# Rows written before the second experts carry their own shift and inverse deviation, and six row gathers go ahead of the six record gathers

## The chip, the cores and the metric

The kernel runs on one core of a Trainium2 chip. The metric is the device time of one execution in microseconds (us); the time of a kernel is the median over several runs. Five engines work beside each other: PE multiplies matrices (PEld loads its weights), DVE and ACT do elementwise work, POOL does small elementwise work and issues the indirect transfers (gathers and scatters), SP issues the plain ones. They meet only at semaphores: an instruction waits until a counter has reached a value.

## The reference

The input is 4096 tokens of 256 numbers. Three blocks follow each other, each on the layer norm of its input and added to it:

```python
x = L0_attn_u
x = x + 0.5 * _L0_ffn_ref(_layernorm(x), Wr, W1, b1, W2, b2)   # mixture of 8 experts
x = x + _L0_attn_ref(_layernorm(x), A_real, A_imag, B, C)      # a linear recurrence over the tokens
x = x + 0.5 * _L0_ffn_ref(_layernorm(x), Wr, W1, b1, W2, b2)   # the same experts again
# _layernorm: (x - mean) / sqrt(var + 1e-5)
# _L0_ffn_ref: the router picks argmax(x @ Wr) of 8 experts and the largest softmax probability p;
#              out = p * (gelu(x @ W1[e] + b1[e]) @ W2[e] + b2[e])
# _L0_attn_ref: h_t = a * h_{t-1} + B u_t (128 complex states), y_t = Re(C h_t)
```

## The kernel before, in words

Tokens are sorted by expert. Each of the two expert stages (`ph` 1 and 2) works through `NT` = 39 tiles `q` of up to 128 sorted tokens: a gather fetches the tile's rows into `xg[q % 6]`, a second gather fetches four numbers for each token, its record (shift, inverse deviation, half the probability), into `recf[:, q % 6]`. Then, for each tile, ACT normalises (`norm`), PE turns the tile (`turn_tile`), ACT and DVE scale and split it into two half-precision parts (`high_x`, `split_x`), PE multiplies by the first weights (`product1`), ACT applies gelu, DVE splits again (`split_h`), PE multiplies by the second weights (`product2`), DVE adds bias and the old row (`result`), and POOL scatters the new rows to DRAM. `RING` = 6 gathers are in flight. `result(q)` writes into `og[q % 2]`, so it waits until the scatter of tile q-2 has landed.

Between the two expert stages lies the recurrence, over 8 chunks `c` of 512 tokens (4 columns of 128 tokens each): SP loads the rows that the first experts wrote (`x1_dram`, rows of `RW` = 258 numbers: the last two are the mean and variance), DVE runs the scan, `add_y(c)` adds the output to the rows in `xs` (for the last chunk ACT does, in `squares`), ACT takes sums of squares (`squares(c)`), and SP stores the new rows to `x2_dram` as soon as they are added (`s_x2`). POOL makes the scan's carried state after each chunk, and in `second_norm` the inverse deviation (a `pow`) and the shift. These stand in `records`, which DVE completes with the probability (`route_weigh`) and SP stores (`store_records`). `route_odds` on DVE waits for `second_norm` of all tokens.

The order on each engine is the order in which the code is written. Toward the second experts it is this. POOL: `second_norm` of the last chunk (after `tile_slots(2)`), then in `ffn` the wait for the sorted order (`sorted_sb`) and for all stores of rows (`s_stored`), and then in pairs the row gather and the record gather of tiles 0 to 5; the first record gather waits for the stored records:

```python
                    for to, source, index in ((xg[k], table, 0), (recf[:, k, :], rec_dram[ph], 1)):
                        if index == 1 and q == 0:
                            pool.wait_ge(s["sorted_all"], 1)
                            pool.wait_ge(s["rec_stored"], 16)
```

Both gathers of a tile count on one semaphore, and `norm(q)` waits for both. PE meanwhile runs matrix products whose results nobody reads (`idle`, L1178): 12 of them after `route_sort(2)`, 5 after the first `turn_tile`.

## Time and profile before

| what | value |
| --- | --- |
| median of 3 runs (lowest to highest) | 613.54 us (612.56 to 614.28) |
| time of the profiled execution | 613.17 us |
| its span | 611.4 us |
| PE busy | 551.8 us (90% of the span) |
| DVE busy | 467.6 us (76%) |
| ACT busy | 409.8 us (67%) |
| POOL busy | 288.1 us (47%) |
| first experts, all 39 tiles | from about 93 us to 306 us of the span |
| recurrence and second routing | about 306 us to 397 us |
| second experts | about 397 us to the end |

The time is 1.8 us more than the span; what lies around the span is not in the trace. A busy share is an average over stages. What an edit is worth is read at the place where it sits: which wait ends last there, and what runs meanwhile.

### The profile page before, as it was taken

To read this page: it belongs to the slowest core of one execution; us is meant where nothing else is said; L and a number is where in the kernel's file an instruction comes from. 1 tells how busy PE (TensorE), PEld (TensorE's weight loads), DVE (VectorE), ACT (ScalarE), POOL (GpSimd) and SP (SyncE) were. 2 spreads that over 40 slices of the span, in tenths; PEclk is the share of its full clock that TensorE was granted. 3 is DMA by queue.
4 is the path that set the end of the run, shared out by engine and by line. 5 is a ranking of instruction groups with operands and counts; after the bars stand their busy time and mean duration, and the time that the engine had idled before them with its cause. 6 is when DMAs were issued, how large, how long until landed. Compare 5 with 4: busy or idle time off the path is not lost.

```text
span 611.4 us, 18700 instructions
## 1 busy us (share of the span) xinstructions
PE 551.8 (90%) x6548; PEld 508.6 (83%) x6548; DVE 467.6 (76%) x1007; ACT 409.8 (67%) x966; POOL 288.1 (47%) x326
## 2 busy tenths in 40 slices
PE   5992158999999999999989989699999999999996
PEld 5991047999999999999977767699999999999996
DVE  5789997888887788877749998666677666666674
ACT  3899977676667776676455662387766677766763
POOL 0025075655655555653245142655555555545532
PEclk9555569999999999999999996799999999999999
DMA  7999112211111121111081223111111112111210
GB/s 250 369 370 378 33 26 97 62 47 55 54 45 55 37 52 44 46 47 36 16 278 35 93 80 104 58 46 54 52 48 53 51 48 45 46 46 46 52 30 15
DMA packets 34873, 51.94 MB, mean 85 GB/s; under 512 B 6747, under 2 KB 27933, under 8 KB 34528
## 3 DMA queue, kind: packets, MB, share of 16 engines
q1 hardware_dynamic: 24800, 31.93, 15.3%
q0 software_dynamic: 9984, 18.83, 11.4%
q8 instruction: 56, 0.92, 0.6%
q14 instruction: 33, 0.27, 0.2%
HBM read 37.98 MB, written 14.59 MB: 86 GB/s over the span
## 4 chain that ended last, share of the span: by engine, by line
PE 67%; DVE 11%; issue 6%; DMA 6%; SPq 4%; POOL 4%; ACT 1%; POOLq 0%; DVEq 0%; ACTq 0%
PE banks L1270 30%; PE banks L1292 10%; PE banks L1293 10%; PE banks L1294 10%; DVE weights_arena L1124 3%; PE banks L1245 3%; DMA weights_arena<-L_attn_u 2%; PE banks L1200 2%; SPq L330 2%; DMA weights_arena<-x_after_ffn 2%; DVE weights_arena L1133 1%; POOL weights_arena L424 1%; DVE weights_arena L1121 1%; SPq L313 1%; DVE weights_arena L1105 1%
## 5 line engine op out<-in xcount | busy, mean ns | idle before, releaser
L617 ACT ACTIVATE weights_arena<-banks,b1t,inv 128x128 f32<-128x128 f32 (+7 forms) x624 | 220.1, 459 | 31.3 <-PE banks L1270 31.2
L1270 PE MATMUL banks<-weights_arena 128*128 128x128 f16 (+7 forms) x3744 | 207.0, 215 | 1.2 <-DVE weights_arena L950 1.1
L1270 PEld LDWEIGHTS banks<-weights_arena 128*128 x3744 | 199.9, 98 | 3.5 <-issue 2.5
L1292 PE MATMUL banks<-weights_arena 128*128 (+7 forms) x624 | 170.3, 273 | 0.2 <-issue 0.2
L1294 PE MATMUL banks<-weights_arena 128*128 (+7 forms) x624 | 170.2, 273 | 0.0
L1293 PE MATMUL banks<-weights_arena 128*128 (+7 forms) x624 | 170.2, 273 | 0.0
L964 DVE TENSOR_SCALAR weights_arena<-weights_arena,hscale 128x512 f16<-128x512 f32 (+5 forms) x156 | 74.7, 479 | 76.0 <-ACT weights_arena L617 75.2
L967 DVE SCALAR_TENSOR_TENSOR weights_arena<-weights_arena,hscale 128x512 f16<-128x512 f32 (+5 forms) x156 | 109.9, 704 | 5.6
L591 ACT ACTIVATE weights_arena<-banks,xscale 128x256 f16<-128x256 f32 (+7 forms) x78 | 35.5, 455 | 90.7 <-PE banks L1245 90.7
L424 POOL DMA_INDIRECT recf<-records,sorti x78 | 76.9, 986 | 23.8 <-issue 23.8
L430 POOL DMA_INDIRECT out<-weights_arena,sorti x39 | 39.5, 1014 | 78.4 <-DVE weights_arena L984 70.6
L430 POOL DMA_INDIRECT x_after_ffn<-weights_arena,sorti x39 | 39.9, 1024 | 77.0 <-DVE weights_arena L988 68.6
L1292 PEld LDWEIGHTS banks<-weights_arena 128*128 128x128 f16 (+7 forms) x624 | 62.3, 100 | 7.0 <-issue 0.7
L1294 PEld LDWEIGHTS banks<-weights_arena 128*128 128x128 f16 (+7 forms) x624 | 62.3, 100 | 6.5
L1293 PEld LDWEIGHTS banks<-weights_arena 128*128 128x128 f16 (+7 forms) x624 | 62.3, 100 | 5.7
L424 POOL DMA_INDIRECT weights_arena<-L_attn_u,sorti x39 | 46.2, 1184 | 29.0 <-DVE sorti L928 17.4
L575 ACT ACTIVATE weights_arena<-weights_arena,recf 128x256 f32<-128x256 f32 (+7 forms) x78 | 46.0, 590 | 8.8 <-DMA recf<-records,sorti 8.8
L981 DVE SCALAR_TENSOR_TENSOR weights_arena<-banks,inv,weights_arena 128x256 f32<-128x256 f32 (+7 forms) x78 | 37.6, 483 | 16.1 <-issue 5.9
L424 POOL DMA_INDIRECT weights_arena<-x_after_ssm,sorti x39 | 40.0, 1026 | 15.1 <-issue 11.6
L950 DVE SCALAR_TENSOR_TENSOR weights_arena<-banks,xscale,weights_arena 128x256 f16<-128x256 f32 (+7 forms) x78 | 35.6, 457 | 7.8 <-ACT weights_arena L591 7.0
L984 DVE SCALAR_TENSOR_TENSOR weights_arena<-weights_arena,recf 128x256 f32<-128x256 f32 (+7 forms) x78 | 37.8, 484 | 2.8
L729 DVE SCALAR_TENSOR_TENSOR weights_arena<-weights_arena,wscale 128x2048 f16<-128x2048 f32 x16 | 37.1, 2341 | 2.3 <-ACT weights_arena L516 2.3
(216 smaller groups left out, 639.1 us busy)
## 6 DMA issues: line engine op xcount, KB each, us to landing
weights_arena<-L_ffn_W SPq DMA_DIRECT2D x16, 1024.0 KB, 12.6
weights_arena<-x_after_ffn SPq DMA_DIRECT2D x8, 516.0 KB, 8.4
weights_arena<-L_attn_u SPq DMA_DIRECT2D x8, 512.0 KB, 10.8
x_after_ssm<-weights_arena SPq DMA_DIRECT2D x8, 512.0 KB, 2.9
weights_arena<-L_ffn_b SPq DMA_DIRECT2D x2, 1024.0 KB, 5.2
recf<-records,sorti POOLq DMA_INDIRECT x78, 2.5
weights_arena<-L_attn_u,sorti POOLq DMA_INDIRECT x39, 3.3
x_after_ffn<-weights_arena,sorti POOLq DMA_INDIRECT x39, 2.5
```

Of the source, the lines that this page charges most:

```text
L424: pool.indirect_dma_start(to, None, source, bass.IndirectOffsetOnAxis(ap=sorti[:, slot(q), index:index + 1].bitcast(U32), axis=0)).then_in ...
L430: pool.indirect_dma_start(dst, bass.IndirectOffsetOnAxis(ap=sorti[:, slot(q), 2:3].bitcast(U32), axis=0), og[q % 2] if ph == 1 else og[q % ...
L575: act.activation(xng[q % 2][0:w], xg[q % RING][0:w], ACT.Identity, bias=recf[0:w, q % RING, 0:1], scale=recf[0:w, q % RING, 1:2]).then_inc ...
L617: last = act.activation(hb[q % 2][:, f, 0:width(q)], src, ACT.Gelu, bias=b1t[:, bass.ds(e * FC + f, 1)], scale=inv1[:, bass.ds(e, 1)])
L964: dve.tensor_scalar(hs[q % 2][:, 0, f, of], hb[q % 2][:, f, of], sc, None, ALU.mult) \
L967: dve.scalar_tensor_tensor(hs[q % 2][:, 1, f, of], hb[q % 2][:, f, of], sc, hs[q % 2][:, 0, f, of], ALU.mult, ALU.subtract).then_inc(s["hs ...
L981: dve.scalar_tensor_tensor(o, acc, i2, b2b[0:w, bass.ds(e * D, D)], ALU.mult, ALU.add) \
L984: last = dve.scalar_tensor_tensor(o, o, recf[0:w, q % RING, 2:3], xg[q % RING][0:w], ALU.mult, ALU.add)
L1270: last = pe.matmul(acc[:, f * P:f * P + n_cols], weights[wpart * DC + d], xts[q % 2][:, xpart, d, 0:n_cols], start=(n == 0), stop=(n == 5))
L1292: pe.matmul(acc, hs[q % 2][:, 0, f, of], high, start=(f == 0), stop=False)
L1293: pe.matmul(acc, hs[q % 2][:, 0, f, of], low, start=False, stop=False)
L1294: last = pe.matmul(acc, hs[q % 2][:, 1, f, of], high, start=False, stop=(f == FC - 1))
```

## The change

The rows in `x2_dram` become 258 numbers long: `second_norm` runs once for each chunk and puts shift and inverse deviation behind the chunk's rows in `xs`. SP's store of a chunk waits for it (`s_nb2`) as well. In the second experts `norm` takes both numbers from the gathered row, and so it waits for the row gather alone; the record gathers count on semaphores of their own, and only `result` waits for them (`records_landed`). At the start of the second experts POOL issues six row gathers and then six record gathers. In both stages `og` has six buffers instead of two, and a few buffers have other addresses.

```diff
--- before.py
+++ after.py
@@ -80,7 +80,7 @@
     x1_dram = nc.dram_tensor("x_after_ffn1", [T, RW], F32, kind="Internal").ap()
 
     rec_dram = {ph: nc.dram_tensor(f"records_{ph}", [T, 4], F32, kind="Internal").ap() for ph in (1, 2)}
-    x2_dram = nc.dram_tensor("x_after_ssm", [T, D], F32, kind="Internal").ap()
+    x2_dram = nc.dram_tensor("x_after_ssm", [T, RW], F32, kind="Internal").ap()
     ctx = ExitStack()
     with ctx:
         def sb(name, shape, dt=F32):
@@ -175,12 +175,12 @@
         hb = [view(k * 1024, FC, P) for k in range(2)]
         b2b = view(2048, E * D)
         hs = [view(4096 + k * 1024, 2, FC, P, dt=F16) for k in range(2)]
-        og = [view(6144 + k * RW, RW) for k in range(2)]
-        xg = [view(8192 + k * D, D) for k in range(RING)]
-        xng = [view(9728 + k * D, D) for k in range(2)]
+        og = [view(6144 + k * RW, RW) for k in range(RING)]
+        xg = [view(8192 + k * RW, RW) for k in range(RING)]
+        xng = [view(10752 + k * D, D) for k in range(2)]
         xts = [view(10240 + k * 256, 2, DC, P, dt=F16) for k in range(2)]
 
-        outcols = [view(6912 + k * D, DC, P) for k in range(2)]
+        outcols = [view(12288 + k * D, DC, P) for k in range(2)]
 
         xs = view(0, NJ, RW)
         uns = [view(NJ * RW + k * CT * D, CT, D) for k in range(2)]
@@ -248,6 +248,8 @@
                 "xt_hi xt m1 gelu h_hi hsplit m2 o_chain o").split()}
             S[ph]["gath"] = [sem(f"gath{k}_{ph}") for k in range(RING)]
             S[ph]["scat"] = [sem(f"scat{k}_{ph}") for k in range(RING)]
+        row_gath = {1: S[1]["gath"], 2: S[2]["gath"]}
+        record_gath = {1: S[1]["gath"], 2: S[1]["gath"]}
         s_load = [sem(f"s_load{k}") for k in range(NC)]
         s_nb, s_un, s_ut, s_uts, s_g, s_mod, s_hr, s_y, s_lg, s_nm, s_x2, s_sq, s_nb2, s_scan, s_neg, s_lx, s_prod, s_state, s_ext = (
             sem(n) for n in ("s_nb s_un s_ut s_uts s_g s_mod s_hr s_y s_lg s_nm s_x2 s_sq s_nb2 s_scan s_neg s_lx s_prod s_state s_ext").split())
@@ -282,6 +284,10 @@
         def in_slot(k):
 
             return len(range(k, NT, RING))
+
+        def records_landed(q):
+
+            return 32 * in_slot(q % RING) + 16 * (q // RING + 1)
 
         def weight_parts(e, which):
 
@@ -367,7 +373,8 @@
                 sp.dma_start(xs[:, c * CT:(c + 1) * CT, :], x1_chunks[c]).then_inc(s_load[c], 16)
             for c in range(NC):
                 sp.wait_ge(s_x2, c + 1)
-                sp.dma_start(x2_chunks[c], xs[:, c * CT:(c + 1) * CT, 0:D]).then_inc(s_stored[2 * c // NC], 16)
+                sp.wait_ge(s_nb2, c + 1)
+                sp.dma_start(x2_chunks[c], xs[:, c * CT:(c + 1) * CT, :]).then_inc(s_stored[2 * c // NC], 16)
                 if c == NC - 2:
                     load_b2(2)
             store_records(2)
@@ -412,31 +419,41 @@
                     for k in range(2):
                         pool.wait_ge(s_stored[k], 16 * (NC // 2))
 
-                def fetch(q):
-
-                    k = q % RING
+                def fetch_rows(q):
+
                     if q >= RING:
                         pool.wait_ge(s["o"], q - RING + 1)
-                    for to, source, index in ((xg[k], table, 0), (recf[:, k, :], rec_dram[ph], 1)):
-                        if index == 1 and q == 0:
-                            pool.wait_ge(s["sorted_all"], 1)
-                            pool.wait_ge(s["rec_stored"], 16)
-                        pool.indirect_dma_start(to, None, source, bass.IndirectOffsetOnAxis(
-                            ap=sorti[:, slot(q), index:index + 1].bitcast(U32), axis=0)).then_inc(s["gath"][k], 16)
+                    to = xg[q % RING][:, 0:D] if ph == 1 else xg[q % RING]
+                    pool.indirect_dma_start(to, None, table, bass.IndirectOffsetOnAxis(
+                        ap=sorti[:, slot(q), 0:1].bitcast(U32), axis=0)).then_inc(row_gath[ph][q % RING], 16)
+
+                def fetch_records(q):
+
+                    if q == 0:
+                        pool.wait_ge(s["sorted_all"], 1)
+                        pool.wait_ge(s["rec_stored"], 16)
+                    pool.indirect_dma_start(recf[:, q % RING, :], None, rec_dram[ph], bass.IndirectOffsetOnAxis(
+                        ap=sorti[:, slot(q), 1:2].bitcast(U32), axis=0)).then_inc(record_gath[ph][q % RING], 16)
 
                 def scatter(q):
 
                     pool.wait_ge(s["o"], q + 1)
                     pool.indirect_dma_start(dst, bass.IndirectOffsetOnAxis(ap=sorti[:, slot(q), 2:3].bitcast(U32), axis=0),
-                                            og[q % 2] if ph == 1 else og[q % 2][:, 0:D], None, bounds_check=T - 1, oob_is_err=False) \
+                                            og[q % RING] if ph == 1 else og[q % RING][:, 0:D], None, bounds_check=T - 1, oob_is_err=False) \
                         .then_inc(s["scat"][q % RING], 16)
 
                 for q in range(RING):
-                    fetch(q)
+                    fetch_rows(q)
+                    if ph == 1:
+                        fetch_records(q)
+                if ph == 2:
+                    for q in range(RING):
+                        fetch_records(q)
                 for q in range(NT):
                     scatter(q)
                     if q + RING < NT:
-                        fetch(q + RING)
+                        fetch_rows(q + RING)
+                        fetch_records(q + RING)
 
             tile_slots(1)
             ffn(1, u, x1_dram)
@@ -452,11 +469,14 @@
                 pool.tensor_tensor(nb[:, of], nb[:, of], rs[:, of], ALU.mult).then_inc(s_nb, 1)
                 pool.tensor_tensor(sd[:, of], rs[:, of], var1[:, of], ALU.mult).then_inc(s_nb, 1)
 
-            def second_norm(of):
-
+            def second_norm(c):
+
+                of = slice(c * CT, (c + 1) * CT)
+                pool.wait_ge(s_sq, c + 1)
                 chain.link(pool.tensor_scalar(m2[:, of], m2[:, of], 1.0 / D, EPS, ALU.mult, ALU.add))
                 chain.link(pool.tensor_tensor(rstd[:, of], m2[:, of], mhalf[:, of], ALU.pow))
-                pool.tensor_tensor(shift[:, of], nmean[:, of], rstd[:, of], ALU.mult).then_inc(s_nb2, 1)
+                pool.tensor_copy(xs[:, of, D + 1], rstd[:, of])
+                pool.tensor_tensor(xs[:, of, D], nmean[:, of], rstd[:, of], ALU.mult).then_inc(s_nb2, 1)
 
             zr, zi = zz[:, 0, CH - 1:CH], zz[:, 1, CH - 1:CH]
             cl, sl = turn[:, 0, CH - 1:CH], turn[:, 1, CH - 1:CH]
@@ -474,14 +494,12 @@
                 pool.tensor_tensor(state[:, 1:2], ev[:, 19:20], ev[:, 21:22], ALU.subtract).then_inc(s_state, 1)
                 if c == 0:
                     inverse_deviations(len(BATCHES) - 1)
-                if c == NC - 3:
-                    pool.wait_ge(s_sq, NC // 2)
-                    second_norm(slice(0, NJ // 2))
-            pool.wait_ge(s_sq, NC - 1)
-            second_norm(slice(NJ // 2, NJ - CT))
+                if c >= 2:
+                    second_norm(c - 2)
+            second_norm(NC - 3)
+            second_norm(NC - 2)
             tile_slots(2)
-            pool.wait_ge(s_sq, NC)
-            second_norm(slice(NJ - CT, NJ))
+            second_norm(NC - 1)
             ffn(2, x2_dram, out)
 
 
@@ -570,10 +588,12 @@
 
                     if q >= 2:
                         act.wait_ge(s["turned"], q - 1)
-                    act.wait_ge(s["gath"][q % RING], q // RING * 32 + 32)
+                    act.wait_ge(s["gath"][q % RING], (q // RING + 1) * (32 if ph == 1 else 16))
                     w = width(q)
-                    act.activation(xng[q % 2][0:w], xg[q % RING][0:w], ACT.Identity, bias=recf[0:w, q % RING, 0:1],
-                                   scale=recf[0:w, q % RING, 1:2]).then_inc(s["xn"], 1)
+                    row = xg[q % RING][0:w]
+                    moments = recf[0:w, q % RING, 0:2] if ph == 1 else row[:, D:RW]
+                    act.activation(xng[q % 2][0:w], row[:, 0:D], ACT.Identity, bias=moments[:, 0:1],
+                                   scale=moments[:, 1:2]).then_inc(s["xn"], 1)
 
                 experts = {}
 
@@ -834,7 +854,7 @@
             def route_odds(ph):
 
                 s = S[ph]
-                dve.wait_ge(a_nb if ph == 1 else s_nb2, 1 if ph == 1 else 3)
+                dve.wait_ge(a_nb if ph == 1 else s_nb2, 1 if ph == 1 else NC)
                 dve.tensor_tensor(je(rt[0]), je(rt[0]), over_e(rstd), ALU.mult).then_inc(s["diff"], 1)
 
             def route_count(ph):
@@ -973,19 +993,21 @@
                     if q == 0:
                         dve.wait_ge(s["b2in"], 16)
                     dve.wait_ge(s["m2"], q + 1)
-                    if q >= 2:
-                        dve.wait_ge(s["scat"][(q - 2) % RING], (q - 2) // RING * 16 + 16)
+                    if q >= RING:
+                        dve.wait_ge(s["scat"][q % RING], q // RING * 16)
+                    if ph == 2:
+                        dve.wait_ge(record_gath[ph][q % RING], records_landed(q))
                     w = width(q)
-                    o, acc = og[q % 2][0:w, 0:D], bank[4 + q % 2][0:w, 0:D]
+                    o, acc = og[q % RING][0:w, 0:D], bank[4 + q % 2][0:w, 0:D]
                     i2 = inv2[0:w, bass.ds(e, 1)]
                     dve.scalar_tensor_tensor(o, acc, i2, b2b[0:w, bass.ds(e * D, D)], ALU.mult, ALU.add) \
                         .then_inc(s["o_chain"], 1)
                     dve.wait_ge(s["o_chain"], q + 1)
-                    last = dve.scalar_tensor_tensor(o, o, recf[0:w, q % RING, 2:3], xg[q % RING][0:w], ALU.mult, ALU.add)
+                    last = dve.scalar_tensor_tensor(o, o, recf[0:w, q % RING, 2:3], xg[q % RING][0:w, 0:D], ALU.mult, ALU.add)
                     if ph == 1:
                         link(last)
                         link(dve.bn_stats(stats[0:w, q % 2, :], o))
-                        last = dve.bn_aggr(og[q % 2][0:w, D:D + 2], stats[0:w, q % 2, :])
+                        last = dve.bn_aggr(og[q % RING][0:w, D:D + 2], stats[0:w, q % 2, :])
                     last.then_inc(s["o"], 1)
 
                 for q in range(3):
```

The order of instructions moves at three places. First POOL, from the last `second_norm` on: `records` is shift and inverse deviation, `x_after_ssm` is `x2_dram`, `recf` takes the record gathers, `sorti` holds the indices. Before:

```order
L405 TENSOR_SCALAR weights_arena<-weights_arena 128x40 [waits pool_chain]
L457 TENSOR_SCALAR m<-m 128x4 [waits s_sq]
L458 TENSOR_TENSOR records<-m,mhalf 128x4 [waits pool_chain]
L459 TENSOR_TENSOR records<-nmean,records 128x4 [waits pool_chain]
L424 DMA weights_arena<-x_after_ssm,sorti 128x256 [waits s_stored1,s_stored0,sorted_sb_2]
L424 DMA recf<-records,sorti 128x4 [waits rec_stored_2,sorted_all_2]
L424 DMA weights_arena<-x_after_ssm,sorti 128x256
```

After:

```order
L412 TENSOR_SCALAR weights_arena<-weights_arena 128x40 [waits pool_chain]
L476 TENSOR_SCALAR m<-m 128x4 [waits s_sq]
L477 TENSOR_TENSOR records<-m,mhalf 128x4 [waits pool_chain]
L478 COPY weights_arena<-records 128x4 [waits pool_chain]
L479 TENSOR_TENSOR weights_arena<-nmean,records 128x4
L427 DMA weights_arena<-x_after_ssm,sorti 128x258 [waits s_stored1,s_stored0,sorted_sb_2]
L427 DMA weights_arena<-x_after_ssm,sorti 128x258 x5
L435 DMA recf<-records,sorti 128x4 [waits rec_stored_2,sorted_all_2]
L435 DMA recf<-records,sorti 128x4 x5
L441 DMA out<-weights_arena,sorti 4096x256 [waits o_2]
```

The last `second_norm` is one copy longer, and all six row gathers now stand ahead of the instruction that waits for the stored records. The five `second_norm`s of the earlier chunks, not shown, moved into the loop over the chunks, each after the state of the chunk two further on.

Second SP's queue over the recurrence: loads of rows, stores of rows, the bias `b2`, records. Before:

```order
L367 DMA weights_arena<-x_after_ffn 128x4x258 x7
L370 DMA x_after_ssm<-weights_arena 128x4x256 [waits s_x2] x7
L357 DMA weights_arena<-L_ffn_b 128x2048 [waits s_sq,s_stored0]
L370 DMA x_after_ssm<-weights_arena 128x4x256 [waits s_x2]
L361 DMA records<-records 128x128 [waits rec_ready_2]
```

After:

```order
L373 DMA weights_arena<-x_after_ffn 128x4x258 x7
L377 DMA x_after_ssm<-weights_arena 128x4x258 [waits s_nb2,s_x2] x7
L363 DMA weights_arena<-L_ffn_b 128x2048 [waits s_sq,s_stored0]
L377 DMA x_after_ssm<-weights_arena 128x4x258 [waits s_nb2,s_x2]
L367 DMA records<-records 128x128 [waits rec_ready_2]
```

Each store has one more wait, on POOL; nothing changes places.

Third DVE at the end of the first experts, the last two calls of `result` (tiles 37 and 38; `m2` is PE's second product, `scat` a landed scatter). Before:

```order
L981 ISA [waits scat5_1,m2_1]
L981 SCALAR_TENSOR_TENSOR weights_arena<-banks,inv,weights_arena 96x256
L984 SCALAR_TENSOR_TENSOR weights_arena<-weights_arena,recf 96x256 [waits o_chain_1]
L987 BN_STATS stats<-weights_arena 96x6 [waits dve_chain]
L988 BN_AGGR weights_arena<-stats 96x2 [waits dve_chain]
L981 ISA [waits scat0_1,m2_1]
L981 SCALAR_TENSOR_TENSOR weights_arena<-banks,inv,weights_arena 16x256
```

After:

```order
L1003 ISA [waits scat1_1,m2_1]
L1003 SCALAR_TENSOR_TENSOR weights_arena<-banks,inv,weights_arena 96x256
L1006 SCALAR_TENSOR_TENSOR weights_arena<-weights_arena,recf 96x256 [waits o_chain_1]
L1009 BN_STATS stats<-weights_arena 96x6 [waits dve_chain]
L1010 BN_AGGR weights_arena<-stats 96x2 [waits dve_chain]
L1003 ISA [waits scat2_1,m2_1]
L1003 SCALAR_TENSOR_TENSOR weights_arena<-banks,inv,weights_arena 16x256
```

Each waits for another scatter: tile 37 waited for that of tile 35 and now waits for that of tile 31, tile 38 for that of tile 32 in place of 36.

## Rows read from the trace of the kernel before

**Rows 1.** Stage table: stretch, its length, busy us by engine, PE clock, DMA.

```profile
397.00:600.00 203.00, 202.88 (x2809) 191.43 (x2809) 138.29 (x263) 143.04 (x380) 108.37 (x109) 1.00 0.17 46
```

**Rows 2.** Chain that ended last, 284 to 312 us: start, us, what.

```profile
303.64 2.11 DMA x_after_ffn<-weights_arena,sorti
305.86 0.38 SPq L367
```

**Rows 3.** Timeline of DVE: start, us, instruction, idle before and releaser.

```profile
299.52 0.48 DVE L981 SCALAR_TENSOR_TENSOR weights_arena<-banks,inv,weights_arena 96x256 f32<-96x256 f32 x1 [1.86 <-DMA x_after_ffn<-weights_arena,sorti]
301.22 0.47 DVE L981 SCALAR_TENSOR_TENSOR weights_arena<-banks,inv,weights_arena 16x256 f32<-16x256 f32 x1
...
606.39 0.47 DVE L981 SCALAR_TENSOR_TENSOR weights_arena<-banks,inv,weights_arena 16x256 f32<-16x256 f32 x1 [1.71 <-PE banks L1294]
```

**Rows 4.** Timeline of PE, last product of tile 38 in each expert stage.

```profile
300.46 0.27 PE L1294 MATMUL banks<-weights_arena 128*16 x1
...
605.94 0.27 PE L1294 MATMUL banks<-weights_arena 128*16 x1
```

**Rows 5.** Chain that ended last, 381 to 402 us.

```profile
386.97 0.21 POOL records L459
...
387.21 0.42 DVE weights_arena L838
...
390.21 0.20 DVE sorti L928
390.41 0.28 issue
390.69 0.46 POOL weights_arena L424
...
392.13 2.19 DMA recf<-records,sorti
...
394.33 0.61 ACT weights_arena L575
```

**Rows 6.** Timeline of PE before the second experts.

```profile
389.17 5.27 PE L1178 MATMUL banks<-iota_r,ident 128*128 128x128 f32 x24
394.99 0.44 PE L1245 MATMUL banks<-ident,weights_arena 128*128 128x128 f32 x2 [0.54 <-ACT weights_arena L575]
```

**Rows 7.** Timeline of SP, the last store of rows.

```profile
381.21 0.36 SPq L370 DMA_DIRECT2D x_after_ssm<-weights_arena x1
```

**Rows 8.** Tile `x_after_ssm`, 325 to 390 us: the eight stores of rows.

```profile
DMA to landing us min/median/max: 2.8/2.9/5.0
```

**Rows 9.** DMA, 335 to 341 us: queue (packets, MB, share), issue (us to landing).

```profile
q8 instruction: 1, 0.02, 1.9%
...
x_after_ssm<-weights_arena SPq DMA_DIRECT2D x1, 512.0 KB, 5.0
```

**Rows 10.** The same view, 363 to 368 us.

```profile
q8 instruction: 1, 0.02, 1.3%
...
x_after_ssm<-weights_arena SPq DMA_DIRECT2D x1, 512.0 KB, 4.2
```

**Rows 11.** The same view, 387.9 to 389.9 us: all packets of this stretch.

```profile
DMA packets 1, 0.02 MB, mean 8 GB/s; under 512 B 0, under 2 KB 0, under 8 KB 0
```

**Rows 12.** DMA, 380 to 402 us: the first row gathers.

```profile
weights_arena<-x_after_ssm,sorti POOLq DMA_INDIRECT x5, 2.8
```

**Rows 13.** Timeline of POOL: norm of 16 columns, state of chunk 6, norm of 4 columns.

```profile
356.82 0.94 POOL L457 TENSOR_SCALAR m<-m 128x16 f32<-128x16 f32 x1 [0.67 <-ACT banks L659]
...
362.97 0.19 POOL L474 TENSOR_TENSOR state<-ev 128x1 f32<-128x1 f32 x1
...
385.40 1.49 POOL L458 TENSOR_TENSOR records<-m,mhalf 128x4 f32<-128x4 f32 x1
```

**Rows 14.** Timeline of DVE: turn of the last chunk, which needs that state.

```profile
365.32 1.22 DVE L1121 TENSOR_TENSOR weights_arena<-turn,banks 128x1024 f32<-128x1024 f32 x1
```

**Rows 15.** Stage table around the start of the second experts.

```profile
391.00:393.00 2.00, 2.00 (x12) 2.00 (x11) 1.09 (x4) 0.00 (x0) 1.70 (x2) 0.50 0.22 59
395.00:397.00 2.00, 1.54 (x12) 1.35 (x12) 0.48 (x1) 0.47 (x1) 1.53 (x2) 1.00 0.28 71
```

## The prediction

> **What bounds the kernel now.** I read the stage table first: within the second experts PE is busy 202.88 of 203.00 us at the full granted clock [rows 1], so nothing that the change does to gathers or buffers inside a stage can save time there. What is left are the seams, where the chain of waits leaves PE. There are two that the change touches. The first is the end of the first experts: the chain runs over the landing of a scatter to DVE's `result(37)` and `result(38)`, over the last scatter, which lands at 303.64 + 2.11 = 305.75, and to SP's first load at 305.86 [rows 2, 3]. The second is the start of the second experts: last `second_norm` on POOL until 387.18, `route_odds`, sorting, the sorted order at 390.41, a row gather, the record gather of tile 0, which starts at 392.13 and lands at 394.32, and ACT's first `norm` at 394.33 [rows 5]. PE's first turn follows at 394.99, after 0.54 us of idleness [rows 6]. All terms below are worked out on the clock of this trace; they add.
>
> **End of the first experts: -0.3.** `result(37)` stood 1.86 us waiting for the scatter of tile 35 [rows 3]. With six buffers it waits for one landed long ago, so it starts when PE has delivered, and is out of the way of `result(38)`. That one can then start when PE's last product is there. PE's last matmul ended at 300.46 + 0.27 = 300.73 [rows 4]. How long DVE needs from there is to be seen at the end of the second experts, where nothing else holds it: 605.94 + 0.27 = 606.21 to 606.39, so 0.18 [rows 3, 4]. 300.91 instead of 301.22 is 0.31 earlier. Scatter, landing and SP's loads all hang on it in the chain [rows 2]. Of the 1.86 us only this is left, because PE is late next. Ends: nothing (if the loads gain nothing from starting earlier) and -0.5 (no latency at all, 301.22 - 300.73). At the end of the second experts nothing is gained: `result(38)` there waited 1.71 us for PE, not for a scatter [rows 3].
>
> **Recurrence: 0.** The old norm of 16 columns sat in front of the state of chunk 6 from 356.82 on; that state was done at 363.16 and DVE asked for it only at 365.32 [rows 13, 14], 2.2 us of slack even then. The new norms have 4 columns; the `pow` of one takes 1.49 us [rows 13], with the smaller instructions about 2.5 us, one per chunk, each behind the state it could delay. Even if each instruction ran at the price of the 0.94 row instead of a few tenths, it would be shorter than the old one from 356.82. If that cover were gone, every microsecond of late state would move the kernel by one. SP's later stores and the bias load behind them are not needed before the first gather and the first `result`. Ends: 0 and 0.
>
> **Last norm: +0.2 on what follows it.** One copy of 4 columns is added, priced as the neighbouring instruction of that shape, 0.21 [rows 5]. DVE's `route_odds` starts 0.02 us after the old end, so sorting and everything behind it on DVE and PE moves with it: the sorted order comes at 390.6, and POOL, which needed 0.28 us from there to its gather [rows 5], could issue at 390.9.
>
> **The last store of rows: the term on which the sum turns.** It went out at 381.21 [rows 7], 0.03 us after ACT's copy; it was more than 6 us ahead of being needed. Now it waits for the shift and goes out at 387.4. Of the eight stores the median landed 2.9 us after issue [rows 8]: 390.3, just ahead of the sorted order at 390.6, so hidden by 0.3 us. But one took 5.0 and one 4.2. The two have something in common: in their stretch lies a packet of the instruction queue, 0.02 MB [rows 9, 10]. The stretch in which the new store would move its data, from half a microsecond after its issue to half a microsecond before the usual landing (387.9 to 389.9), has today exactly one packet, 0.02 MB [rows 11], the size of that kind. PE's instructions are the same in number and order after the change, and at that point PE waits for DVE, so the packet should move with them by the same 0.2 us and meet the store. Then the landing takes 4.2 to 5.0 us; I take the middle, 4.6, between the two. 387.4 + 4.6 = 392.0; POOL's gather starts 0.28 later, at 392.3; the row gather lands 2.8 us later [rows 12], at 395.1, against 394.32 for the record of today. `norm` takes 0.61, and PE's turn moves from 394.99 to 395.7: **+0.7**. Ends: landing 2.9 and 5.0.
>
> The Trainium skill speaks against this term: in "Runtime: NRT & Kernel Launch", section "Instruction fetch mechanics", an engine's instructions come in 16 KiB blocks over a DMA queue of its own, and the cost of crossing to the next block is called mostly hidden. By that rule the store would land as the median does. The two slow stores say otherwise for a transfer that shares the time with such a block, and "DMA: Bandwidth & Descriptors", section "Why a DMA increments its semaphore by 16 and not by 1", gives a reason that fits them: a transfer is spread over up to 16 engines and counts as landed only with the last one. By the first rule alone the sum would be that of the first rival below; by the rows it is the one forecast.
>
> **What the gain would have been.** Leaving the record out of `norm`'s wait takes away 1.44 us between the two gathers (390.69 to 392.13) and changes a 2.19 us landing for one of 2.8 [rows 5, 12]: without the store's delay the row is there at 390.9 + 2.8 = 393.7 and normalised at 394.3. PE could not use all of it: its 24 idle passes, at a granted clock of 0.50 [rows 15], ended at 394.44 [rows 6] and now end 0.2 later, 394.6. So the turn would come at 394.6 and not at 394.99, **-0.35**. These passes cap the step.
>
> **Records: 0.** The record of tile 0 is now the seventh gather, 6 x 1.44 = 8.6 us after the first, so at 400.9, and lands about 2.2 later at 403.1 [rows 5]. `result(0)` follows three half tiles of PE's work: 203 us hold some 37 tiles [rows 1], so 5.5 each, 397.8 + 8.2 = 406. If this cover of 3 us were gone, DVE would hold `product2(2)` through the bank, not earlier. Further down one more wait for each `result` lies in DVE's idle time, except in the last one, where it may cost 0.05.
>
> **Sum.** -0.3 + 0 + 0.7 + 0.05 = +0.4 on the profiled execution's 613.17 (span 611.4 and 1.8 around it): **613.6 us**. The median of the runs shown, 613.54, lies 0.4 above that execution, so the same sum on the median would be 614.0; 613.6 is as good as these can tell apart. 0.3% of the time, what a measurement of this kernel can tell from no change, is 1.84 us.
>
> **Rivals.** *First: the store is hidden after all* (the packet comes earlier or later than the store's data, or costs nothing). Then -0.31 - 0.35 + 0.05 = -0.6: 612.6. For it: the median of the eight stores, 2.9, hardly above the least, 2.8 [rows 8]; against it: the packet in the stretch. The edge is a landing of about 3.8 us: below it PE's turn is earlier than today, above it later. A mild form of this is that the change doesn't do what it says: rows go ahead, but PE's idle passes end only 0.5 us before today's turn, so there is little to win in any case.
>
> *Second, on the slower side: the new wait lowers PE's clock.* Between the idle passes and the first turn PE now stands 1.1 us in place of 0.54. The granted clock was 0.50 (the lower of the two levels, 1.2 GHz) over 391 to 393 and 1.00 over 395 to 397 [rows 15]. If it fell again at the longer gap for about the length of the idle passes, which ran at that level for 5 us [rows 6], PE would do half its work in them: 2.5 us, with the 0.4 of the sum 616.1. The point from which it decides is whether the clock falls at all after 395. Against it: five more idle matmuls follow the first turn at once.
>
> *Third: more is won than I see*, for instance if, with the first seam's wait gone, all of its 1.86 us [rows 3] came back and the store were hidden too: -1.86 - 0.35 = -2.2, 611.0. Against it stands PE's last product at 300.73.
>
> **How the numbers follow.** The forecast 0.62, first rival 0.25, second 0.07, third 0.06. Range of the likeliest: landing 4.2 gives +0.0, 5.0 gives +0.8, a gain of nothing at the first seam +0.3 more, so 613.2 to 614.3; with the scatter of runs (612.56 to 614.28 for one kernel) and the first rival, 611.9 to 614.8. Faster by over 0.3% needs 611.7: the third rival and a little of the first, 0.07. Slower needs 615.4: the second rival and a little more, 0.08. Within 0.3%: 0.85.
>
> **What would show it.** Right: `result(37)` without a wait for a scatter and SP's first load 0.3 us earlier; a last store that lands over 4 us after issue, with an instruction packet in its stretch; POOL's first row gather released by the store and not by the sorted order; PE's first turn more than 0.54 us after the idle passes. Wrong: a landing of 2.9 (then 612.6), a granted clock below 1.00 after the first product, or a wait of `result` for a record.

## The result, and the profile after

The changed kernel took **616.0 us** (median of five executions, 613.66 to 617.71), beside 613.5 us (612.56 to 614.28) for the kernel before on the same chip: ratio 1.004, 95% interval 1.002 to 1.0059. That is 2.5 us above the median of before. The profiled execution took 615.49 us with a span of 613.1, against 613.17 and 611.4.

The chain of waits of the changed kernel, 284 to 320 us and then 375 to 415 us (start, us, what), answers to [rows 2, 5]:

```profile
304.20 2.11 DMA x_after_ffn<-weights_arena,sorti
306.43 0.38 SPq L373
...
386.13 1.50 POOL records L477
387.69 0.19 POOL weights_arena L478
387.88 0.18 POOL weights_arena L479
388.13 4.08 DMA x_after_ssm<-weights_arena
392.27 0.76 issue
393.03 2.92 DMA weights_arena<-x_after_ssm,sorti
395.98 0.61 ACT weights_arena L595
396.63 0.45 PE banks L1267 x2
```

DVE and the sorting have left the chain. It now runs from POOL's last norm to SP's store, through a landing of 4.08 us, to POOL, to the landing of the first row gather, to ACT and PE. The timelines say the same from the engines' side (start, us, instruction, idle time before and its releaser): DVE's `result(37)`, its two `result(38)`, the gather, PE's idle passes and PE's first turn; they answer to [rows 3, 6].

```profile
299.08 0.48 DVE L1003 SCALAR_TENSOR_TENSOR weights_arena<-banks,inv,weights_arena 96x256 f32<-96x256 f32 x1 [0.52 <-PE banks L1316]
301.79 0.47 DVE L1003 SCALAR_TENSOR_TENSOR weights_arena<-banks,inv,weights_arena 16x256 f32<-16x256 f32 x1 [1.04 <-PE banks L1316]
...
608.04 0.47 DVE L1003 SCALAR_TENSOR_TENSOR weights_arena<-banks,inv,weights_arena 16x256 f32<-16x256 f32 x1 [1.72 <-PE banks L1316]
...
393.03 1.12 POOL L427 DMA_INDIRECT weights_arena<-x_after_ssm,sorti  x1 [4.98 <-DMA x_after_ssm<-weights_arena]
...
390.06 5.39 PE L1200 MATMUL banks<-iota_r,ident 128*128 128x128 f32 x24
396.63 0.44 PE L1267 MATMUL banks<-ident,weights_arena 128*128 128x128 f32 x2 [1.19 <-ACT weights_arena L595]
```

The DMA view of the changed kernel, 387 to 389 us (packets; queue with packets, MB, share; issue with KB and us to landing), answers to [rows 9, 10]:

```profile
DMA packets 1, 0.02 MB, mean 8 GB/s; under 512 B 0, under 2 KB 0, under 8 KB 0
...
q8 instruction: 1, 0.02, 3.7%
...
x_after_ssm<-weights_arena SPq DMA_DIRECT2D x1, 516.0 KB, 4.1
```

The instruction packet is there, in the stretch of the store, as forecast. The stage table of the changed kernel (length; busy us of PE, PEld, DVE, ACT, POOL; granted clock; DMA share, GB/s) answers to [rows 1, 15]:

```profile
40.00:78.00 38.00, 12.27 (x79) 10.80 (x79) 35.71 (x73) 35.58 (x32) 12.04 (x9) 1.00 0.64 224
...
395.00:397.00 2.00, 0.81 (x6) 0.60 (x6) 0.00 (x0) 0.60 (x1) 1.39 (x3) 0.94 0.38 114
397.00:600.00 203.00, 202.34 (x2789) 190.93 (x2788) 137.21 (x261) 142.92 (x380) 109.87 (x110) 1.00 0.18 47
```

**Where the time went.** I cut each traced execution at four marks that every kernel has: POOL's first gather of the first experts, DVE's last `result(38)` there, PE's first turn of the second experts, and the last `result(38)`. The lengths are differences of the starts in the timelines; the last 5 us of a span are alike in all.

```
                          to the first   first     from result(38)  second   span
                          gather         experts   to PE's turn     experts
before                    78.21          223.01    93.77            211.40   611.4
changed                   79.10          222.69    94.84            211.41   613.1
before, once more         78.22          222.03    93.83            211.51   610.6
changed, once more        78.69          221.67    95.11            211.44   612.0
```

The third column is the second of the two seams that the prediction spoke of; from here on "the seam" means this column, and "the opening" the first. The seam grew by 1.07 and 1.28 us. The second experts are untouched to 0.1 us. The opening is ahead of everything that the diff touches, and the first experts differ by 1 us between two executions of the same kernel.

### The profile page after: what moved, and what is told of

It reads as the page before. It is cut to its first block, busy times and chain, and to the rows that moved or that the text cites. A ratio compares the mean times of both kernels' runs of the same rounds, so it can differ in the third digit from the quotient of the medians.

```text
span 613.1 us, 18728 instructions
## 1 busy us (share of the span) xinstructions
PE 552.8 (90%) x6548; PEld 510.0 (83%) x6548; DVE 467.7 (76%) x1007; ACT 410.0 (67%) x966; POOL 297.5 (49%) x349
## 4 chain that ended last, share of the span: by engine, by line
PE 75%; DVE 10%; issue 5%; DMA 5%; POOL 4%; SPq 1%; ACT 0%; POOLq 0%; DVEq 0%; ACTq 0%
PE banks L1292 31%; PE banks L1314 11%; PE banks L1316 11%; PE banks L1315 11%; PE banks L1222 4%; PE banks L1267 3%; DVE weights_arena L1146 3%; PE banks L1194 2%; DMA weights_arena<-x_after_ffn 2%; DVE weights_arena L1155 1%; DVE weights_arena L1143 1%; DVE weights_arena L1127 1%; POOL weights_arena L427 1%; DMA recf<-records,sorti 1%; SPq L373 1%
## 5 line engine op out<-in xcount | busy, mean ns | idle before, releaser
L1267 PE MATMUL banks<-ident,weights_arena 128*128 128x128 f32 (+5 forms) x156 | 29.8, 272 | 6.7 <-ACT weights_arena L595 6.7
```

The costliest lines, as they stand in the source:

```text
L1267: last = pe.transpose(bank[6 + q % 2][:, d * P:d * P + w], xng[q % 2][0:w, d * P:(d + 1) * P], ident[0:w, 0:w])
```

## The experiments

The kernels ran in three batches, each with the kernel before beside it on the same chip: medians 613.51 (35 executions), 613.45 (29) and 613.40 (28). Ratios are to these, with the 95% interval in brackets.

**Each kernel once more.** No edit to either.

> The kernel before, once more, for two things: how far two sets of runs of one kernel lie apart, and whether the opening of the kernel, ahead of anything the change touches, differs from execution to execution. The trace of the changed kernel is 0.9 us late already at the end of the entry's matmuls (first gather 79.10 against 78.21). If that is a difference between executions, this kernel shows it too in some of its own: ratio 1.000, but spans that come in two groups about 0.9 us apart, and its granted clock over the whole span in two groups too (0.93 and 0.98). If it is a property of the changed kernel, this one stays with the one group: 611 us of span, 0.93.

> The changed kernel, once more. Theory A (the last store's landing is the whole of the change's cost): first gather of the second experts released by the store, landing 3.4 to 4.2 us after issue, PE's first turn about 1.1 us later than before relative to the opening; time +0.8 us over before when both openings are alike, up to +1.7 when they are not. Theory B (something in the change costs the opening 0.9 us as well): all its executions have the first gather of the first experts at 79.1 and none at 78.2.

Before: 613.20, ratio 1.0002 [0.9989, 1.0014]. Changed: 614.84, ratio 1.004 [1.0024, 1.0056], 613.59 to 618.16. The slowdown is there again, but smaller in its median: 1.3 us above the kernel before beside it, not 2.5.

The reason is in the list of executions. By their mean granted clock over the span they fall into three groups, whatever the kernel. All executions of the two kernels for which I have that clock (before: its three sets and the repetition; changed: the first five and the repetition), median and number:

```
              A: 0.921 to 0.935    B: 0.975 to 0.982    C: 0.983 to 0.99
before        612.91 (65)          615.35 (10)          614.10 (29)
changed       613.98 (8)           616.83 (6)           615.49 (3)
difference    +1.1                 +1.5                 +1.4
```

From here on "A 612.73 (8)" stands for the median in group A and the number of executions. Within each group the change costs 1.1 to 1.5 us. The changed kernel's few executions make these differences rough: drawing its executions and before's anew at random puts the one in A between 0.8 and 2.0 us and those in B and C between 0.5 and 3.1. The border between B and C (0.982 and 0.983) is drawn close; A stands apart. Of before's 104 executions 39 lie in B and C, of the first five of the changed kernel four did, three of them in B. That mix lifted its median to 616.0; with the mix of the repetition it was 614.8.

The mean is not what PE lived through in the opening. This is the opening of the kernel before in the stage table:

```profile
40.00:78.00 38.00, 11.39 (x75) 9.91 (x75) 36.30 (x77) 36.49 (x33) 12.04 (x9) 0.50 0.63 223
```

And a run of eight equal matmuls there, in its timeline of PE:

```profile
72.53 0.45 PE L1231 MATMUL banks<-weights_arena 128*128 128x40 f16 x8 [0.15 <-DVE weights_arena L896]
```

The same run in the timeline of the changed kernel, whose row of the table, shown above, reads 1.00:

```profile
72.82 0.45 PE L1253 MATMUL banks<-weights_arena 128*128 128x40 f16 x8 [0.15 <-DVE weights_arena L916]
```

Eight matmuls take 0.45 us at a recorded clock of 0.50 and at one of 1.00. They do depend on the clock: the same run takes 0.37 us ahead of the second experts in the kernel with its gathers in pairs, where the record reads 1.00 (390 to 392 us), and the run of 16 ahead of it takes 0.96 us in the opening of the changed kernel and 0.57 at 387.65 us. So in C (and in B) the record of the opening does not tell what PE ran at; the clock was at its lower level (1.2 GHz) in both. What differs in time is the opening, which ends at 78.9 to 79.3 us in six traces of B and C and at 78.2 to 78.7 in the seven of A (without the kernel whose opening was changed, below); why, no run shows. In B the clock also falls at the start of the recurrence; that is shown below, in the kernel with its gathers in pairs.

**The store of the last chunk split in two.** Its rows go out when they are ready, as in the kernel before; the two moments of each row (shift and inverse deviation) follow in a transfer of 4 KB behind the last norm, and only this one waits for the norm.

```diff
             for c in range(NC):
                 sp.wait_ge(s_x2, c + 1)
+                if c == NC - 1:
+                    sp.dma_start(x2_chunks[c][:, :, 0:D], xs[:, c * CT:(c + 1) * CT, 0:D]).then_inc(s_stored[1], 16)
                 sp.wait_ge(s_nb2, c + 1)
-                sp.dma_start(x2_chunks[c], xs[:, c * CT:(c + 1) * CT, :]).then_inc(s_stored[2 * c // NC], 16)
+                part_of_row = slice(0 if c + 1 < NC else D, RW)
+                sp.dma_start(x2_chunks[c][:, :, part_of_row], xs[:, c * CT:(c + 1) * CT, part_of_row]) \
+                    .then_inc(s_stored[2 * c // NC], 16)
...
-                        pool.wait_ge(s_stored[k], 16 * (NC // 2))
+                        pool.wait_ge(s_stored[k], 16 * (NC // 2 + k))
```

> The changed kernel, but of the last chunk the rows are stored as soon as they are added, as before the change, and only their shift and inverse deviation (8 bytes a row) in a second store behind the last norm. Theory A: that small store has no 516 KB to move and little on any one engine for an instruction packet to hold up; it lands about 2 us after issue, so before or at the sorted order, and the first row gather goes out 0.3 us behind that. The turn of PE then follows its idle passes with next to no gap: 1.2 to 1.4 us less than the changed kernel, 0.5 below before for like openings. Rival (a store's landing is a fixed cost, not its bytes, or 512 pieces of 8 bytes are slow): it lands after 3 us or more and wins less than 0.5 us.

613.04, ratio 1.0000 [0.9984, 1.0016]; A 612.73 (8), B 616.60 (1), C 614.51 (3). The seam is 93.54, 1.3 to 1.6 shorter than in the changed kernel. The time is that of before, not the 0.5 below it that was expected. The landing of the small store in this kernel, tile view, 385 to 390 us:

```profile
DMA to landing us min/median/max: 2.9/2.9/2.9
```

The first gather, the idle passes and the first turn, in its timelines:

```profile
390.67 1.12 POOL L431 DMA_INDIRECT weights_arena<-x_after_ssm,sorti  x1 [3.79 <-DVE sorti L952]
...
388.87 5.44 PE L1204 MATMUL banks<-iota_r,ident 128*128 128x128 f32 x24
394.23 0.44 PE L1271 MATMUL banks<-ident,weights_arena 128*128 128x128 f32 x2
```

The small store landed later than the 2 us expected, and an instruction packet of 0.02 MB lay in its stretch; in the last kernel of this section it landed after 1.8 us with none. The profile names the sorted order as releaser again, but the gather starts 0.57 us behind it and not 0.28, and some 0.9 behind the landing, so the landing may still have held it for 0.3 us. This costs nothing: PE goes from its idle passes straight into the turn. Everything else of the change is in this kernel, so the whole cost of the change sits in the wait of that one store; and this seam, 0.2 below before's, is all that the new order of the gathers can bring under the idle passes.

**A second store ahead of the last one.** The rows of the last chunk are also written to a spare table first, on the same queue.

```diff
+                if c == NC - 1:
+                    sp.dma_start(twin_chunk, xs[:, c * CT:(c + 1) * CT, :]).then_inc(twin_done, 16)
                 sp.dma_start(x2_chunks[c], xs[:, c * CT:(c + 1) * CT, :]).then_inc(s_stored[2 * c // NC], 16)
```

> The changed kernel with the suspected cost enlarged: the last chunk's rows are first stored once more, to a tensor that nobody reads, so the store that POOL waits for moves its data behind 516 KB of other data. Theory A: landing about 1.3 to 1.6 us later than in the changed kernel, PE's first turn later by the same, time +1.3 to +1.6 us over the changed kernel (615.5 to 616 in the group with the lower mean clock). Rival (something else holds the start): less than 0.5 us.

618.83, ratio 1.0079 [1.0054, 1.0104]; A 617.03 (2), B 619.45 (4), so 2.6 to 3.0 us above the changed kernel in either. The chain of this kernel:

```profile
389.91 5.74 DMA x_after_ssm<-weights_arena
395.67 0.04 POOLq L425
395.72 0.76 issue
396.48 2.96 DMA weights_arena<-x_after_ssm,sorti
```

The landing grew by 1.5 to 1.7 and the time followed. It grew by more than that: the store also went out 0.4 us behind its twin, and the second experts took 0.7 us more behind a fall of the clock (below). Together these are 2.6 to 2.8 us.

**Six output buffers alone**, in the kernel before.

```diff
-        og = [view(6144 + k * RW, RW) for k in range(2)]
+        og = [view(6144 + k * RW, RW) for k in range(RING)]
...
-                    if q >= 2:
-                        dve.wait_ge(s["scat"][(q - 2) % RING], (q - 2) // RING * 16 + 16)
+                    if q >= RING:
+                        dve.wait_ge(s["scat"][q % RING], q // RING * 16)
```

> The kernel before with only the six output buffers (and the moved column buffer). Both theories: tile 37's result no longer waits for a scatter, and the last result of the first experts starts 0.3 us earlier relative to the opening; from there all is as before. Theory A: ratio 0.9995, time -0.3 us. Theory B, if the moved buffers are what costs the opening: +0.6 us, first gather at 79.1.

614.08, ratio 1.0008 [0.9995, 1.002]; A 613.50 (6), B 615.60 (1), C 614.39 (5): no gain. In its trace the waits for scatters are gone, as in the changed kernel, and `result(38)` waits 1.04 us for PE. But see DVE in the second trace of the kernel before:

```profile
298.24 0.48 DVE L981 SCALAR_TENSOR_TENSOR weights_arena<-banks,inv,weights_arena 96x256 f32<-96x256 f32 x1 [1.23 <-DMA x_after_ffn<-weights_arena,sorti]
300.25 0.47 DVE L981 SCALAR_TENSOR_TENSOR weights_arena<-banks,inv,weights_arena 16x256 f32<-16x256 f32 x1 [0.34 <-PE banks L1294]
```

`result(37)` waited for a scatter and `result(38)` for PE none the less. The 0.31 us was there in the one execution from which it was read, and not in the next: of four traces with two buffers, two had it (the first, and the wide rows alone) and two did not. Over all traces but that of the kernel with a changed opening, the first experts took 222.0 to 223.0 us with two buffers (four traces, mean 222.6) and 221.7 to 222.8 with six (nine, mean 222.3). A difference of 0.3 is what was forecast, but the spread hides it. Compared within the groups it does not settle either: 222.5 and 221.9 in A (three and four traces), 222.8 and 222.6 in B and C (one and five). A gain of some tenths at this seam is neither shown nor excluded.

**Wide rows alone**, in the kernel before: rows of 1032 bytes in place of 1024, the last two numbers unread, the store where it was.

```diff
-    x2_dram = nc.dram_tensor("x_after_ssm", [T, D], F32, kind="Internal").ap()
+    x2_dram = nc.dram_tensor("x_after_ssm", [T, RW], F32, kind="Internal").ap()
...
-                sp.dma_start(x2_chunks[c], xs[:, c * CT:(c + 1) * CT, 0:D]).then_inc(s_stored[2 * c // NC], 16)
+                sp.dma_start(x2_chunks[c], xs[:, c * CT:(c + 1) * CT, :]).then_inc(s_stored[2 * c // NC], 16)
...
```

The hunks left out widen the buffers of the gathered rows to match.

> The kernel before with rows of 258 numbers in the tensor between recurrence and second experts (the last two hold stale mean and variance, which nobody reads), stored and gathered with them, and nothing else. All stores that meet no instruction packet landed 3.3 to 3.5 us after issue in the changed kernel and 2.8 to 2.9 before. Theory: those 0.5 us are the price of rows of 1032 bytes, so they appear here too, off the chain, and the time is that of before (ratio 1.000). Rival: they come from when the stores go out (behind POOL's norm, beside other work); then these land in 2.9.

613.94, ratio 1.0012 [0.9991, 1.0033]; A 612.78 (3), B 615.72 (3), C 613.94 (4), those of before to 0.4. The eight stores of this kernel, tile view, 325 to 390 us; [rows 8] has them for 1024 bytes:

```profile
DMA to landing us min/median/max: 3.1/3.7/5.0
```

In both kernels two of the eight stores shared their stretch with an instruction packet. The other six landed after 2.8 to 3.3 us in the kernel before (median 2.9) and after 3.1 to 4.4 in this one (median 3.6); the last one after 2.9 and 3.7. So stores of these wider rows land some 0.7 us later. It need not be the eight bytes that are moved: in the kernel with the split store the last chunk's rows went out as 1024 bytes each, to places 1032 bytes apart, and landed after 3.8 us, with no packet in the stretch, where the same rows to places 1024 bytes apart took 2.9. That is one landing, and no run takes the two apart further. The delay costs the kernel nothing as long as the store has 6 us of slack, and is part of the price once it has none.

**The gathers in pairs again**, in the changed kernel: row and record of tile 0, then of tile 1, and so on.

```diff
                 for q in range(RING):
                     fetch_rows(q)
-                    if ph == 1:
-                        fetch_records(q)
-                if ph == 2:
-                    for q in range(RING):
-                        fetch_records(q)
+                    fetch_records(q)
```

> The changed kernel with the six row gathers and six record gathers at the start of the second experts in pairs again; norm still waits for the row alone. Theory A: the order is worth nothing, since tile 0's row is the first gather either way and PE does not need tile 1's row earlier than 2.5 us after it: time that of the changed kernel. Rival (the order is what helps or hurts): 0.5 us or more apart from it.

615.93, ratio 1.0036 [1.0017, 1.0054]; A 613.79 (3), B 617.58 (5), C 615.46 (2), in A and C the changed kernel's to 0.2. With the store as the releaser the order of the gathers is worth nothing. Its trace, one of group B, had what the prediction's second rival described. PE's idle passes, its first turn and the last `result(38)`, in the timelines of this kernel:

```profile
391.24 2.92 PE L1196 MATMUL banks<-iota_r,ident 128*128 128x128 f32 x24
398.33 0.44 PE L1263 MATMUL banks<-ident,weights_arena 128*128 128x128 f32 x2 [4.17 <-ACT weights_arena L591]
...
610.73 0.47 DVE L999 SCALAR_TENSOR_TENSOR weights_arena<-banks,inv,weights_arena 16x256 f32<-16x256 f32 x1 [1.71 <-PE banks L1312]
```

Three rows of its stage table:

```profile
312.00:330.00 18.00, 16.03 (x78) 10.54 (x78) 10.62 (x15) 11.11 (x22) 13.25 (x25) 0.91 0.49 157
...
398.00:400.00 2.00, 1.67 (x11) 1.67 (x12) 0.46 (x1) 0.76 (x2) 1.39 (x3) 0.78 0.25 70
400.00:402.00 2.00, 2.00 (x18) 1.73 (x17) 0.03 (x1) 0.60 (x1) 1.70 (x2) 0.50 0.22 51
```

Two things are to be seen. The clock stood at 0.91 over 312 to 330 us; it does so in the three traces of B (this one, the six buffers alone, the second store) and reads 1.00 in all others. It is not of the change's making: with six buffers alone the last norm ended 87.45 us behind `result(38)`, against 85.96 before. The other is the start of the second experts. The passes ran at the full clock and were over in 2.92 us, PE then stood for 4.17 us, and the clock was at 0.50 at 400 to 402 us, with PE already in the experts' products. From the first turn to the last `result` it took 212.40 us, against 211.40 to 211.51 in every trace without this fall. That may be why its B is 0.75 above the changed kernel's. The changed kernel has no trace in B. With six buffers alone, also traced in B, the pause was 3.03 us and the seam 95.33; here they are 4.17 and 96.53. So the store's wait adds 1.2 us to the seam in B as well, and the fall is likely in the changed kernel's own executions of B, but no trace shows it.

**The 12 idle passes behind the sort taken out**, in the kernel before, to have a price for that fall. The 5 behind the first turn stay.

```diff
-                if ph == 2:
-                    idle(12, bank[2])
```

> The kernel before without the 12 idle matmuls behind the second sort, to price the clock at the start of the second experts by itself. PE then stands still for over 5 us ahead of its first turn. Theory on the clock: the granted clock is at 0.50 when the second experts begin, and from PE's first turn to the last result 1 us or more is lost against the 211.4 us of the kernels that start at 1.00; time +1 to +3 us. Rival: the clock rises as before, nothing is lost.

614.50, ratio 1.0016 [1.0004, 1.0029]; A 613.64 (4), 0.7 above before's; B 614.88 (4), 0.5 below; C 614.50 (2), 0.4 above. The first turn and the passes behind it, in its timeline of PE:

```profile
394.85 0.69 PE L1243 MATMUL banks<-ident,weights_arena 128*128 128x128 f32 x2 [5.78 <-ACT weights_arena L575]
395.33 2.34 PE L1178 MATMUL banks<-iota_r,ident 128*128 128x128 f32 x10
```

The clock there, in its stage table:

```profile
396.00:398.00 2.00, 2.00 (x15) 1.94 (x14) 0.48 (x1) 0.75 (x2) 1.50 (x2) 0.53 0.25 65
```

The second experts took 212.09 us, 0.7 more, as the times of the trace's own group, A. The kernel with the second store shows the same, 212.10, behind a pause of 3.44 us.

**More idle passes**, in the changed kernel: 15 in place of 12 ahead of the experts.

```diff
-                    idle(12, bank[2])
+                    idle(15, bank[2])
```

> The changed kernel with 15 idle matmuls behind the sort instead of 12, so that PE has hardly a pause (1.2 to 1.7 us in the traces) ahead of its first turn. If the new pause sometimes lowers the granted clock at the start of the second experts (the rival on the slower side), the executions of 617 to 618 us go, and the median of the group with a mean clock over 0.95 falls by 1 us or more. If the clock has no part in it: the same times, or up to 0.3 us more where the passes end behind the row.

614.43, ratio 1.0016 [0.9999, 1.0032]; A 614.08 (9), C 616.17 (3), none in B. PE's gap fell to 0.44 us, and A stayed where it was (613.98): in that group the gap has no price of its own. The lower median comes from the shares of the groups. The last store landed after 3.9 us here, with an instruction packet in its stretch as in the changed kernel.

**The instruction packet moved away from the store.** 96 counter increments on a semaphore that nobody waits for stand at PE's start; in a second version they stand ahead of the first experts, where PE is idle.

```diff
+            for _ in range(96):
+                pe.sem_inc(pad, 1)
             pe.wait_ge(const_done, 2)
```

```diff
+                if ph == 1:
+                    for _ in range(96):
+                        pe.sem_inc(pad, 1)
                 pe.wait_ge(s["vals"], 1)
```

> The changed kernel with 96 counter increments put ahead of PE's first wait, where PE stands idle for its parameters. They cost nothing, but PE's later instructions lie 96 places further on in its 16 KB blocks, so the block that is fetched while the last store moves is fetched somewhere else. Theory A with the packet as part of the cost: no instruction packet in the last store's stretch, landing 3.3 to 3.4 us after issue in place of 4.1 to 4.3, PE's first turn 0.8 us earlier, time 0.8 us less than the changed kernel (like with like in the granted clock). Rival (the packet only happens to lie there): landing 4.1 to 4.3 as before, time unchanged.

> The experiment with shifted blocks again, with the 96 counter increments where PE stands idle for 18 us, ahead of the first routing's sort (at the very start they held up the entry by 8 us). Theory A: the last store meets no instruction packet, lands 3.4 us after issue and not 4.1 to 4.3, and PE's first turn of the second experts stands 0.7 us closer to the last result of the first experts (94.1 to 94.4 us instead of 94.8 to 95.1); time 0.7 us under the changed kernel's, like group with like. Rival: another packet takes its place, or the landing stays over 4.

The first was badly placed: 623.32, ratio 1.0146 [1.012, 1.0172]. The increments took PE's time where it was wanted, and its first matmul came at 15.60 us and not at 6.12. Its time says nothing on the packet; its landing does, 3.5 us with no packet in the stretch. The second: 614.54, ratio 1.0014 [1.0002, 1.0027]; A 614.45 (7), B 615.06 (3), C 614.90 (2). Its DMA view, 388 to 392 us:

```profile
q1 hardware_dynamic: 672, 0.59, 44.3%
issues: line engine op xcount, KB each, median us to landing
x_after_ssm<-weights_arena SPq DMA_DIRECT2D x1, 516.0 KB, 3.6
```

No instruction packet, and a landing of 3.6 where the changed kernel had 4.1 and 4.3. From the store to PE's turn it took 8.08 us, against 8.50 and 8.75. So the packet costs this landing 0.5 to 0.8 us against the changed kernel's two traces; against all four traces that have the packet there (3.9 to 4.5, with the more idle passes and the pairs) it is 0.3 to 1.1. The price is rough: this kernel's store at 353.8 us landed after 3.6 with a packet in its stretch, and stores of the changed kernel's second trace with none after 3.3 to 4.2.

The kernel did not become shorter for it: A is 0.5 above the changed kernel's, B and C are 1.8 and 0.6 below with few executions, and the seam is 95.15 and not the 94.1 to 94.4 expected. SP's first loads came 5.30 us behind the last `result(38)` of the first experts and not 4.64 as in the changed kernel. The cause is in the chain of this kernel, 300.5 to 307 us, and its DMA view, 303.8 to 306.6:

```profile
303.78 2.77 DMA x_after_ffn<-weights_arena,sorti
...
q8 instruction: 1, 0.02, 2.4%
```

The last scatter of the first experts lands after 2.77 us, with an instruction packet in its stretch. In the first version it lands after 2.68, with one as well; in the twelve other traces it lands after 2.10 or 2.11 with none. The increments moved a packet away from the store and another one onto this scatter, where it cost 0.66 us of the same chain. So a packet costs time at two places, and what moving them gained at one was lost at the other.

**Moments apart, and `route_odds` later**, to win what the first experiment left: DVE does the two `route_rows` steps ahead of `route_odds`, which waits for POOL's norm, so that less stands behind that norm.

```diff
             route_tiles(2)
-            route_odds(2)
             route_rows(2, 2)
             route_rows(2, 3)
+            route_odds(2)
```

> The experiment with the last chunk's moments stored apart, with DVE's route_odds behind the last two route_rows instead of ahead of them, so that neither PE's sort nor its idle passes hang on POOL's last norm. DVE no longer waits 0.4 us for POOL there nor spends 0.4 us on the odds first, so the sort and the sorted order come 0.5 to 0.9 us earlier; the small store (landing 2.9 us) then holds the first row gather. Turn 0.1 to 0.5 us earlier than in that experiment, time 612.5 in the group with the lower mean clock, which beats both kernels. If the small store's landing holds everything: no gain.

A miss. The profiled execution took 612.39, as expected, with a seam of 93.57; but the median was 615.64, ratio 1.0029 [1.0014, 1.0045]; A 613.95 (3), B 616.18 (4), C 614.99 (4), each 0.8 to 1.0 above before's. The sorted order did not come earlier but 0.3 us later (89.7 us behind `result(38)`, against 89.4 in the first experiment). The end of POOL's last norm in the two timelines shows where the gain went, first here and then in the first experiment:

```profile
386.18 0.55 POOL L482 COPY weights_arena<-records 128x4 f32<-128x4 f32 x1
386.70 0.65 POOL L483 TENSOR_TENSOR weights_arena<-nmean,records 128x4 f32<-128x4 f32 x1
...
386.52 0.19 POOL L482 COPY weights_arena<-records 128x4 f32<-128x4 f32 x1
386.67 0.20 POOL L483 TENSOR_TENSOR weights_arena<-nmean,records 128x4 f32<-128x4 f32 x1
```

These two instructions took 1.2 us beside DVE's `route_rows` and 0.4 us while DVE stood waiting for them. Behind them DVE then waited 0.57 us for ACT, a wait that other work covered before. PE's gap ahead of the first turn had grown from nothing to 2.19 us, because its idle passes started earlier and ended sooner. Why the median is above before's I can't say; I suspect the fall of the clock in the executions that weren't traced, but the one trace doesn't show it. No version was measurably better than the kernel before.

## Why the prediction was wrong

**First seam, -0.3.** The mechanism is as forecast: `result(37)` waits for no scatter, and `result(38)` starts 0.17 behind PE's last matmul. On the profiled execution the first experts were 0.32 shorter. But before's own second trace was 0.98 shorter without the change, and the buffers alone gained nothing that can be measured. A gain read from one execution was less than the difference between two; whether some tenths of it are real stays open.

**Recurrence, records, second experts: 0.** Right. The second experts took 211.40 before and 211.41 after, and no `result` waited for a record.

**The last norm and the last store: +0.7.** The step was right in each link, and its size too small: +1.07 and +1.28. The store went out 86.34 us behind `result(38)`, 0.16 more than worked out. From there to PE's turn I had 8.3 us and 8.50 and 8.75 were measured. The landing was shorter than the 4.6 taken, 4.1 and 4.3. Against that POOL needed 0.82 us from the landing to its gather and not 0.28, and the gather landed after 2.9 to 3.0 and not 2.8. The 0.28 was the time behind a wait for DVE [rows 5]; behind the store's landing it was 0.82 or 0.83 in every kernel in which the store released the gather. Of the landing, 2.9 is the usual store [rows 8], some 0.7 the wider rows, which I had not priced at all, and the rest, 0.5 to 0.8, the instruction packet. So the 4.6 came near in part by luck: it left out the wider rows and put the packet at 1.7 (4.6 less 2.9).

The Trainium skill, "Runtime: NRT & Kernel Launch", section "Instruction fetch mechanics", calls the cost of crossing to the next block of instructions mostly hidden. For the engine that fetches this may hold, and no run here tests it; for a transfer that shares the time with the block it does not, by the last store's 3.5 and 3.6 us without a packet against 3.9 to 4.5 with one, and the last scatter's 2.11 against 2.68 and 2.77.

**The first rival**, that the store is hidden, did not come true, and would not have without the packet. Its edge was put at a landing of 3.8. With the measured links it is 3.0: before's seam leaves 93.77 - 86.34 = 7.43 us from store to turn, and the links behind the landing take 8.50 - 4.08 = 4.42. Wide rows alone, at 3.5 to 3.7, are beyond it. **The third** had nothing for it.

**The second rival**, the clock, I gave 0.07. On the trace of the changed kernel it is wrong: 1.00 from 397 on, 211.41 us. But its mechanism exists. Behind pauses of PE of 3.44, 4.17 and 5.78 us (the second store, the pairs, the kernel without the 12 passes) the clock was at 0.50 in the passes behind the first turn, with the pairs into the first products, and the second experts took 0.6 to 1.0 us more. Behind one of 3.03 us (the six buffers alone) they took 211.44, as usual. In the changed kernel the pause was 1.19 and 1.68 in its two traces. Both lie outside B; in B it was probably longer, as said with the pairs, but that isn't shown.

**The step that failed is the last one of the sum**, in which one profiled execution was taken as good for the median, and 612.56 to 614.28 as the scatter of this kernel. The two seams alone were also mis-sized, the last store +1.07 to +1.28 and not +0.7, the first seam nothing measurable and not -0.3; but with these the sum put on before's median gives 614.6 to 614.8, still inside the range. What lay outside it was the scatter. The kernel's executions fall into three groups with medians 2.4 us apart, and three times did not show how far the upper ones reach (to 615.8). The change costs 1.1 to 1.5 within a group. The seam's +1.07 and +1.28 account for that in A, and in B and C for all but 0.2 to 0.4, which three and six executions cannot tell from nothing. The rest of the measured 616.0, some 1.1, is four of five executions in B and C. Whether the change itself makes B more frequent stays open: 6 of its 17 executions lie there, against 10 of 104 before; with three idle passes more, which alter nothing ahead of the recurrence's end, none of 12. The edited kernels that leave the last store as it was before have it too, wide rows alone in 3 of 10 and the kernel without the 12 passes in 4 of 10.

## What to carry to other kernels

Before a producer is made to wait for one more input, look at whether its transfer had slack: here a 516 KB store that was 6 us ahead of need was put on the critical path for the sake of 4 KB, and sending the 4 KB alone took the cost away. Instructions added to one engine also shift which transfers an instruction packet meets: look at every transfer on the chain, not only at the one that was to be freed. Price a wait for a landing by a wait for a landing, not by a wait for an engine. A sum over one profiled execution has the error of that execution: with only that to go by, leave room in the range for what two executions of one kernel differ by, here 1 us in one stage and 2.4 us between the medians of the groups.
